# Quartering the value weights of an attention and experts kernel and loading them ahead of a block of x

## Chip, cores and metric

One core of a Trainium2 chip. The metric is the device time of one execution in microseconds (us); less is better.

## What is computed

One transformer layer on x of 2048 rows by 512 columns, in f32: attention and then a mixture of experts, each followed by a residual sum and a layer norm. Only the start matters here, the projections:

```python
q = (x @ Wq + bq).reshape(B, T, H, HD)
k = (x @ Wk + bk).reshape(B, T, HKV, HD)
v = (x @ Wv + bv).reshape(B, T, HKV, HD)
```

H is 16, HKV is 4 and HD is 128, so that Wv is 512 by 512.

## The kernel before, in words

`stage_project` is the first of the stages; after it come attention, the router, the experts and the last layer norm. Each of the five engines has one instruction stream, and semaphores join them. Within a stream the order is written by hand and is strict: an instruction behind a wait does not start before that wait is met.

**The split.** Each f32 matrix product is done as three products of halves: every operand is split into a high part, a rounded copy (ScalarE, `nc.scalar.copy`), and a low part, the value less its high part (VectorE, a subtraction). TensorE sums low by high, high by low and high by high in PSUM.

**The blocks.** x goes through in 16 blocks of 128 rows, called block 0 to block 15 below. For each, SyncE loads it (256 KB) into `xraw[k]`, k being the block's parity; TensorE transposes it in four pieces (`transposes`, L234, instructions at L239); ScalarE writes the high part (`x_hi`, L305, instruction at L311); VectorE the low part (`x_lo`, L392, L394) and keeps it for the later stage (`keep_lo`, L397, L399); GpSimd keeps the high part (`keep_hi`). Then twelve products with the value weights follow (`project_v`, L242, at L248), a bias (L405), a split (L317, L409) and a store of 512 KB (`store_v`, L177).

**The value weights.** `wv_raw` is 128 by 2048: four chunks of 512 columns, one for each 128 columns of x. It is loaded in two halves of 512 KB (L170), split in two halves (L324 and L417), and the products of block 0 are written by themselves (`project_first`, L252, at L258 with the high parts of the weights and at L263 with the low ones).

**TensorE's order at the start** (L267 to L275): 7 matmuls on zeros that keep the array busy (`keep_busy`, L103, each showing as two instructions of the trace at L106), transposes of blocks 0 and 1, 15 more `keep_busy`, the products of block 0, the transposes of block 2, the products of block 1. Then a loop: transposes of block 3, products of 2, transposes of 4, products of 3, and so on.

**SyncE's order** (L165 to L192): the identity (64 KB), blocks 0 and 1 of x, the two halves of the value weights, the bias `bv_b` (256 KB); blocks 2 and 3, each behind a wait for the transposes of the block that held its buffer (`xt_done`, L174); two head weights `w_raw` (257 KB each), `cosT` and `sinT` (1024 KB each), the mask (64 KB); and in a loop from there block 4, the store of block 0's values, block 5, the store of block 1's values, and so on. `load_x(4)` waits for three transposed blocks. The tables `cosT` and `sinT` are first read at L444, in the stage's second part, which starts at 60 us.

Of the kernel before, what the change touches and what calls it, by code (L numbers as in the profile page):

```python
# [23 lines left out]
F32 = mybir.dt.float32  # L24
# [5 lines left out]
ALU = mybir.AluOpType  # L30
# [3 lines left out]
P = 128  # L34
T = 2048
C = 512
# [6 lines left out]
NC = C // P  # L43
# [3 lines left out]
HI, LO = 0, 1  # L47
# [55 lines left out]
def keep_busy(nc, n, bank, ident):  # L103

    for _ in range(n):
        nc.tensor.matmul(bank, ident, ident, start=True, stop=True)  # L106


def stage_project(nc, base, own, sems, passed, x, wqk, wv, bv, cos, sin, ident_d, mask_d, qk_d, v_d):
    NH = H + HKV  # L110
    with ExitStack() as ctx:
# [5 lines left out]
        def sem(name):  # L117
            return sems.enter_context(nc.semaphore("p1_" + name))

        ident, maskf, identb, maskb = own.ident, own.maskf, own.identb, own.maskb  # L120
# [3 lines left out]
        xraw = [sb(f"xraw{k}", [P, C], kb=3 + 2 * k) for k in range(2)]  # L124
        xt = [[sb(f"xt{k}{s}", [P, NC, P], F32R) for s in "hl"] for k in range(2)]
        wv_raw = sb("wv_raw", [P, NC * C])
        wv_s = [sb(f"wv{s}", [P, NC * C], F32R) for s in "hl"]
        WV = [slice(s * NC * C // 2, (s + 1) * NC * C // 2) for s in range(2)]
        bv_b = sb("bv_b", [P, C])
        vfull = [sb(f"vfull{k}", [P, C]) for k in range(2)]  # L130
        vout = [sb(f"vout{k}", [P, HKV, 2, HD], F32R) for k in range(2)]
# [18 lines left out]

        x_in = [sem(f"x_in{k}") for k in range(2)]
        ident_in, const_in, bv_in = own.ident_in, sem("const_in"), sem("bv_in")
        wv_in = [sem(f"wv_in{s}") for s in range(2)]
        wv_hi, wv_lo = sem("wv_hi"), sem("wv_lo")
        xt_done, xt_hi, xt_lo = sem("xt_done"), sem("xt_hi"), sem("xt_lo")
        hi_kept, lo_kept = sem("hi_kept"), sem("lo_kept")
# [7 lines left out]

        def sync(sp, preload):  # L165
            sp.dma_start(ident[:], ident_d).then_inc(ident_in, 16)
            for k in range(2):
                sp.dma_start(xraw[k][:], x[k * P:(k + 1) * P, :]).then_inc(x_in[k], 16)
            for s in range(2):
                sp.dma_start(wv_raw[:, WV[s]], wv[:, WV[s]]).then_inc(wv_in[s], 16)  # L170
            sp.dma_start(bv_b[:], bv.partition_broadcast(P)).then_inc(bv_in, 16)

            def load_x(tb, k):
                sp.wait_ge(xt_done, tb - 1)  # L174
                sp.dma_start(xraw[k][:], x[bass.ds(tb * P, P), :]).then_inc(x_in[k], 16)

            def store_v(tb, k):  # L177
                sp.wait_ge(v_lo, tb + 1)
                sp.dma_start(v_d[bass.ds(tb, 1)].rearrange("o j p h d -> p (o j) h d"),
                             vout[k][:].bitcast(F32)).then_inc(v_out[k], 16)  # L180

            for k in range(2):
                load_x(2 + k, k)
            for k in range(2):
                sp.dma_start(w_raw[k][:], wqk[k]).then_inc(w_in[k], 16)
            sp.dma_start(cosT[:], cos).then_inc(const_in, 16)
            sp.dma_start(sinT[:], sin).then_inc(const_in, 16)
            sp.dma_start(maskf[:], mask_d).then_inc(own.mask_in, 16)
            with sp.Fori(2, NB // 2) as i:
                for k in range(2):  # L190
                    load_x(i * 2 + k, k)
                    store_v(i * 2 + (k - 4), k)  # L192
            for tb in range(NB - 4, NB):
                store_v(tb, tb % 2)

            def head_step(i, between=(), last=False):
                for k in range(2):
                    n = i * 2 + k
                    if not last:
                        sp.wait_ge(w_lo, n + 1)  # L200
                        sp.dma_start(w_raw[k][:], wqk[bass.ds(n + 2, 1)].rearrange("o p m -> (o p) m")
                                     ).then_inc(w_in[k], 16)
                    if k < len(between) and between[k]:
                        between[k](sp)
                    for t in range(NT):
                        sp.wait_ge(q_lo, n * NT + (t + 1))
                        sp.dma_start(qk_d[bass.ds(n, 1), :, t].rearrange("o p h t -> (o p) h t"),
                                     qout[k][:, t].bitcast(F32)).then_inc(q_out[k], 16)

            with sp.Fori(0, EARLY // 2) as i:  # L210
                head_step(i)

            def keys(sp):
                for k in range(2):
                    sp.wait_ge(v_out[k], 16 * (NB // 2))
                    sp.wait_ge(q_out[k], 16 * NT * (EARLY // 2))
                preload[0](sp)

            head_step(EARLY // 2, (keys, preload[1]))
            head_step(EARLY // 2 + 1, (preload[2], preload[3]))  # L220
            head_step(EARLY // 2 + 2, (preload[4],))
            with sp.Fori(EARLY // 2 + 3, NH // 2 - 1) as i:
                head_step(i)
            def queries(sp):
                sp.wait_ge(q_out[0], 16 * NT * (NH // 2))
                preload[5](sp)

            head_step(NH // 2 - 1, (None, queries), last=True)
# [4 lines left out]
        def tensor(pe):  # L233
            def transposes(tb, k, i, early):  # L234
                pe.wait_ge(x_in[k], i * 16 + 16)
                if not early:
                    pe.wait_ge(xt_lo, tb - 1)
                for c in range(NC):
                    last = nc.tensor.transpose(pt[k][:, c, :], xraw[k][:, c * P:(c + 1) * P], ident[:])  # L239
                last.then_inc(xt_done, 1)  # L240
# [8 lines left out]
                                                start=(n == 0 and c == 0), stop=(n == 2 and c == NC - 1))  # L249
                last.then_inc(v_mm, 1)  # L250

            def project_first():  # L252
                pe.wait_ge(xt_lo, 1)
                for part in range(2):
                    pe.wait_ge(wv_hi, part + 1)
                    for xs in (HI, LO):
                        for c in range(part * NC // 2, (part + 1) * NC // 2):
                            nc.tensor.matmul(pv[0][:], xt[0][xs][:, c, :], wv_s[HI][:, c * C:(c + 1) * C],  # L258
                                             start=(c == 0 and xs == HI), stop=False)
                for part in range(2):  # L260
                    pe.wait_ge(wv_lo, part + 2)
                    for c in range(part * NC // 2, (part + 1) * NC // 2):
                        last = nc.tensor.matmul(pv[0][:], xt[0][HI][:, c, :], wv_s[LO][:, c * C:(c + 1) * C],  # L263
                                                start=False, stop=(c == NC - 1))
                last.then_inc(v_mm, 1)

            pe.wait_ge(wv_lo, 1)  # L267
            keep_busy(nc, 7, pq[0][:, 0:P], rs[0][:, 0:P])
            pe.wait_ge(ident_in, 16)
            transposes(0, 0, 0, True)  # L270
            transposes(1, 1, 0, True)
            keep_busy(nc, 15, pq[0][:, 0:P], ident[:])
            project_first()
            transposes(2, 0, 1, False)
            project_v(1, 1, True)  # L275
            with pe.Fori(1, NB // 2 - 1) as i:
# [27 lines left out]
        def scalar(act):  # L304
            def x_hi(tb, k, early):  # L305
                act.wait_ge(xt_done, tb + 1)
                if not early:
                    act.wait_ge(v_mm, tb - 1)
                    act.wait_ge(hi_kept, tb - 1)
                    act.wait_ge(lo_kept, tb - 1)  # L310
                nc.scalar.copy(xt[k][HI][:], pt[k][:]).then_inc(xt_hi, 1)  # L311
# [5 lines left out]
                nc.scalar.copy(vout[k][:, :, HI, :], vfull[k][:].rearrange("p (j d) -> p j d", j=HKV)  # L317
                               ).then_inc(v_hi, 1)

            for k in range(2):  # L320
                x_hi(k, k, True)
            for s in range(2):
                act.wait_ge(wv_in[s], 16)
                nc.scalar.copy(wv_s[HI][:, WV[s]], wv_raw[:, WV[s]]).then_inc(wv_hi, 1)  # L324
            for k in range(2):
                x_hi(2 + k, k, False)
                v_hi_part(k, k, 0, True)
# [33 lines left out]
                v_hi_part(NB - 2 + k, k, NB // 2 - 1, False)  # L361
            act.wait_ge(ident_in, 16)
            nc.scalar.copy(identb[:], ident[:]).then_inc(own.mask_ready, 1)
            act.wait_ge(own.mask_in, 16)
            nc.scalar.copy(maskb[:], maskf[:]).then_inc(own.mask_ready, 1)

            def head_step(i, first, last=False):
# [21 lines left out]
        def vector(dve):  # L389
            nc.vector.memset(rs[0][:, 0:P], 0.0).then_inc(wv_lo, 1)  # L390

            def x_lo(tb, k):  # L392
                dve.wait_ge(xt_hi, tb + 1)
                nc.vector.tensor_tensor(xt[k][LO][:], pt[k][:], xt[k][HI][:].bitcast(F32), ALU.subtract  # L394
                                        ).then_inc(xt_lo, 1)

            def keep_lo(tb, k):  # L397
                dve.wait_ge(xt_lo, tb + 1)
                nc.vector.tensor_copy(xT[LO][:, :, bass.ds(tb * P, P)], xt[k][LO][:].bitcast(F32)).then_inc(lo_kept, 1)  # L399
# [9 lines left out]
                nc.vector.tensor_tensor(vout[k][:, :, LO, :], vfull[k][:].rearrange("p (j d) -> p j d", j=HKV),  # L409
                                        vout[k][:, :, HI, :].bitcast(F32), ALU.subtract).then_inc(v_lo, 1)  # L410

            for k in range(2):
                x_lo(k, k)
                keep_lo(k, k)
            for s in range(2):
                dve.wait_ge(wv_hi, s + 1)
                nc.vector.tensor_tensor(wv_s[LO][:, WV[s]], wv_raw[:, WV[s]], wv_s[HI][:, WV[s]].bitcast(F32), ALU.subtract  # L417
                                        ).then_inc(wv_lo, 1)
            dve.wait_ge(bv_in, 16)

            def step(i, first):
# [39 lines left out]
            for k in range(2):  # L461
                v_bias(NB - 2 + k, k, False)
                v_lo_part(NB - 2 + k, k)
            dve.wait_ge(const_in, 32)

            def head_step(i, first, last=False):
                for k in range(2):
# [1782 lines left out]
```

## Time and profile before

| What | us |
|---|---|
| Median of 3 runs | 2062.01 (2060.47 to 2062.39) |
| The profiled execution's own time | 2060.34 |
| Its span in the trace | 2058.5 |
| TensorE busy | 2038.4, 99% of the span |
| VectorE, ScalarE, GpSimd busy | 1691.4, 1400.6, 854.4 |

The span is the part of an execution that the profiler covers. PE is TensorE, PEld its weight loads, DVE is VectorE, ACT is ScalarE, POOL is GpSimd, SPq are the DMA issues of SyncE. A row of the timeline gives the start, the length of the merged stretch, the engine, the line, the tiles and the count; in brackets stands the idle time before it and what ended that. "DMA to landing" is the time from a transfer's issue to its semaphore. Ends of matmuls are modelled, so that the start of the next one is the better measure of what a group takes.

### The profile page before, as it was taken

Reading aid. Unit: us, or ns where it says so; the run is one execution under the profiler, and the core shown is the slowest. Engines: PE = TensorE matmul, PEld = TensorE weight load, DVE = VectorE, ACT = ScalarE, POOL = GpSimd, SP = SyncE. Lnnn points to the kernel's source line nnn. Section 1 sums busy time; section 2 is a strip of 40 time slices with the busy share of each in tenths; the row PEclk is TensorE's granted clock in tenths of the full one; section 3 lists DMA queues with packets and bytes.
Section 4 is the critical chain, followed back from the end, with each engine's and each line's share of the span. In section 5 each row is a group of like instructions: output and inputs, shape, how many; then the busy total and the mean of one; then the engine's idle time right before and its main releaser. Section 6 shows DMA issues by size and latency. Waiting matters only on the chain.

```text
span 2058.5 us, 36148 instructions
## 1 busy us (share of the span) xinstructions
PE 2038.4 (99%) x11961; PEld 1745.4 (85%) x11961; DVE 1691.4 (82%) x3508; ACT 1400.6 (68%) x2726; POOL 854.4 (42%) x812
## 2 busy tenths in 40 slices
PE   9999999999999999999999999999989999999998
PEld 8888888888888888888888888788879999999997
DVE  6899997888778887788877888566678889898886
ACT  3677776776667666677667776433447778777876
POOL 1000023333233332333323333155557777788775
PEclk9999999999999999999999999999999999999999
DMA  7458564011340213402243010567649999999998
GB/s 268 184 219 293 222 233 147 26 72 44 129 146 21 73 53 125 141 21 72 77 170 133 22 72 25 199 244 285 241 158 258 298 295 298 302 288 296 302 292 269
DMA packets 130405, 361.07 MB, mean 175 GB/s; under 512 B 15312, under 2 KB 32208, under 8 KB 125648
## 3 DMA queue, kind: packets, MB, share of 16 engines
q1 hardware_dynamic: 102160, 292.03, 40.1%
q0 software_dynamic: 28096, 67.12, 13.7%
q8 instruction: 85, 1.39, 0.3%
q14 instruction: 64, 0.52, 0.1%
HBM read 224.21 MB, written 134.89 MB: 174 GB/s over the span
## 4 chain that ended last, share of the span: by engine, by line
PE 81%; DVE 3%; ACT 2%; issue 1%; DMA 0%; POOL 0%; DVEq 0%; ACTq 0%; POOLq 0%
PE p_S L724 18%; PE p_O L756 17%; PE p_TP L738 11%; PE p_pgu L1678 9%; PE p_acc L1147 8%; PE p_prest L1678 4%; PE p_py L1695 4%; PE p_tp L1663 3%; PE p_py L1696 1%; PE p_py L1697 1%; ACT p_prob L822 1%; PE p_lg L1169 1%; ACT p_pT1h L830 1%; DVE p_nmax L879 1%; PE p_picked L1708 1%
## 5 line engine op out<-in xcount | busy, mean ns | idle before, releaser
L724 PE MATMUL p_S<-p_kT,p_q 128*128 128x512 f32 (+3 forms) x1920 | 459.6, 369 | 1.0
L724 PEld LDWEIGHTS p_S<-p_kT,p_q 128*128 128x128 f32 x1920 | 333.7, 188 | 66.3 <-ACT p_prob L822 14.7
L948 POOL TENSOR_SCALAR p_prob<-p_prob,p_inv 128x256 f32<-128x256 f32 (+7 forms) x256 | 193.1, 754 | 432.8 <-DVE p_inv L890 432.7
L948 POOL TENSOR_SCALAR p_prob<-p_prob,p_inv,p_part 128x1024 f32<-128x1024 f32 (+1 forms) x128 | 150.8, 1178 | 455.2 <-DVE p_inv L895 455.2
L879 DVE TENSOR_REDUCE p_nmax<-p_S 128x1 f32<-128x1024 f32 (+6 forms) x256 | 253.6, 991 | 80.7 <-PE p_S L724 74.3
L738 PE MATMUL p_TP<-p_ident,p_prob 128*128 128x128 f32 x2176 | 307.6, 273 | 2.0 <-DVE p_pT0l L900 1.1
L738 PEld LDWEIGHTS p_TP<-p_ident,p_prob 128*128 128x128 f32 x2176 | 250.7, 140 | 45.9 <-issue 11.8
L830 ACT CAST p_pT1h<-p_TP 128x512 fp32r<-128x512 f32 (+2 forms) x320 | 164.9, 552 | 98.2 <-PE p_TP L738 98.1
L830 ACT CAST p_pT0h<-p_TP 128x384 fp32r<-128x384 f32 (+3 forms) x320 | 147.8, 498 | 117.3 <-PE p_TP L738 117.1
L1945 POOL DMA_INDIRECT sum_scratch<-p_y,p_tokT x124 | 206.0, 1661 | 42.6 <-issue 37.2
L756 PE MATMUL p_O<-p_pT1h,p_v 128*128 128x512 f32 x584 | 222.1, 411 | 0.4 <-DVE p_pT1l L900 0.2
L822 ACT ACTIVATE p_prob<-p_S,p_nm 128x256 f32<-128x256 f32 (+7 forms) x256 | 189.7, 741 | 38.8 <-DVE p_nm L879 36.1
L900 DVE TENSOR_TENSOR p_pT1l<-p_TP,p_pT1h 128x512 fp32r<-128x512 f32 (+2 forms) x320 | 197.2, 633 | 20.0 <-ACT p_pT1h L830 18.2
L1933 POOL DMA_INDIRECT p_xg<-x_scratch,p_tokT x128 | 168.5, 1317 | 75.0 <-issue 38.1
L756 PE MATMUL p_O<-p_pT0h,p_v 128*128 128x512 f32 x504 | 194.4, 413 | 0.0
L900 DVE TENSOR_TENSOR p_pT0l<-p_TP,p_pT0h 128x384 fp32r<-128x384 f32 (+3 forms) x320 | 175.8, 566 | 13.8 <-ACT p_pT0h L830 13.4
L1147 PE MATMUL p_acc<-p_woh,p_ot 128*128 128x512 f32 x512 | 172.4, 402 | 0.0
L822 ACT ACTIVATE p_prob<-p_S,p_nmax 128x1024 f32<-128x1024 f32 (+1 forms) x128 | 142.4, 1112 | 4.9 <-DVE p_nmax L879 1.8
L879 DVE TENSOR_REDUCE p_nm<-p_S 128x1 f32<-128x128 f32 (+7 forms) x128 | 96.3, 753 | 51.3 <-PE p_S L727 50.5
L756 PEld LDWEIGHTS p_O<-p_pT1h,p_v 128*128 128x128 f32 x584 | 110.0, 188 | 19.4 <-DVE p_pT1l L900 1.4
L1511 POOL TENSOR_SCALAR p_lo_hot<-p_iota_lo,p_lo 128x128 f16<-128x128 f32 x117 | 77.8, 683 | 88.2 <-DVE p_hi L1403 88.2
L756 PE MATMUL p_O<-p_pT1l,p_v 128*128 128x512 f32 x292 | 114.3, 392 | 0.0
(356 smaller groups left out, 4567.0 us busy)
## 6 DMA issues: line engine op xcount, KB each, us to landing
p_w_raw<-in_gu SPq DMA_DIRECT2D x64, 768.0 KB, 7.0
qk_scratch<-p_qout SPq DMA_DIRECT2D x80, 512.0 KB, 2.7
p_q<-qk_scratch SPq DMA_DIRECT2D x16, 2048.0 KB, 8.8
o_scratch<-p_oT SPq DMA_DIRECT2D x64, 512.0 KB, 3.3
p_ot<-o_scratch SPq DMA_DIRECT2D x32, 1024.0 KB, 7.2
p_w_raw<-in_gu SPq DMA_DIRECT2D x64, 256.0 KB, 8.3
v_scratch<-p_vout SPq DMA_DIRECT2D x16, 512.0 KB, 2.9
p_t_raw<-in_dn SPq DMA_DIRECT2D x32, 256.0 KB, 8.0
```

The costliest lines, as they stand in the source:

```text
L724: mm = nc.tensor.matmul(out if k0 // 512 == (k1 - 1) // 512 else out.rearrange("p (n k) -> p n k", n=2), x, y, start=(n == 0), stop=(n == 2))
L738: mm = nc.tensor.transpose(TP[g % 2][:, n, :], prob[u % KEEP][:, s * P:(s + 1) * P], ident[:])
L756: mm = nc.tensor.matmul(O[f % 2][:], x, y, start=(s == 0 and i == 0), stop=(s == nblk(f) - 1 and i == 2))
L822: nc.scalar.activation(prob[k][:, keys(u, a)], S[:, score_cols(u, a)], ACT.Exp, bias=top[:, k:k + 1], accum_out=rsum[:, k, a:a + 1]).then_ ...
L830: nc.scalar.copy(pT[m % 2][HI][:, 0:n, g, :], TP[g % 2][:, 0:n, :]).then_inc(turn_hi, 1)
L879: r = nc.vector.reduce_max(out[:, k:k + 1], S[:, cols], AX_X, negate=True)
L900: nc.vector.tensor_tensor(pT[m % 2][LO][:, 0:n, g, :], TP[g % 2][:, 0:n, :], pT[m % 2][HI][:, 0:n, g, :].bitcast(F32), ALU.subtract).then_ ...
L948: nc.gpsimd.tensor_scalar(prob[k][:, cols], prob[k][:, cols], inv[:, k:k + 1], scale, ALU.mult, ALU.mult).then_inc(normed, 1)
L1147: mm = nc.tensor.matmul(acc[k][:], a, w, start=(n == 0 and m == 0), stop=(n == H - 1 and m == 2))
L1678: mm = nc.tensor.matmul(out, a[:, col:col + P], b[:, d, :], start=(m == 0 and d == 0), stop=(m == 2 and d == NC - 1))
L1933: nc.gpsimd.indirect_dma_start(out=xg[k][c][:], out_offset=None, in_=x1_d, in_offset=bass.IndirectOffsetOnAxis(ap=tokT[:, e, c:c + 1], axi ...
L1945: nc.gpsimd.indirect_dma_start(out=sum_d[k], out_offset=bass.IndirectOffsetOnAxis(ap=tokT[:, e, c:c + 1], axis=0), in_=y[k][c][:], in_offs ...
```

## The change

The value weights are loaded, split and multiplied in four quarters of 256 KB, `WV[c]` now being chunk c. Block 1 of x is loaded behind them. ScalarE and VectorE split block 1 behind the four quarters. TensorE's order becomes: 7 `keep_busy`, transposes of block 0, 8 `keep_busy`, the products of block 0 chunk by chunk (for each chunk two with its high part, and one with the low part of the chunk before), the transposes of block 1 ahead of the last low product, and then transposes of block 2 and products of block 1 as before. SyncE waits for the four high parts (`wv_hi`) ahead of `cosT`. Since quarters 2 and 3 signal `const_in` and `mask_in`, the later waits on these count 16 more. The diff, without its lines of context:

```diff
--- before.py
+++ after.py
...
-        WV = [slice(s * NC * C // 2, (s + 1) * NC * C // 2) for s in range(2)]
+        WV = [slice(c * C, (c + 1) * C) for c in range(NC)]
...
-        wv_in = [sem(f"wv_in{s}") for s in range(2)]
+        wv_in = [sem(f"wv_in{s}") for s in range(2)] + [const_in, own.mask_in]
...
-            for k in range(2):
-                sp.dma_start(xraw[k][:], x[k * P:(k + 1) * P, :]).then_inc(x_in[k], 16)
-            for s in range(2):
-                sp.dma_start(wv_raw[:, WV[s]], wv[:, WV[s]]).then_inc(wv_in[s], 16)
+            sp.dma_start(xraw[0][:], x[0:P, :]).then_inc(x_in[0], 16)
+            for c in range(NC):
+                sp.dma_start(wv_raw[:, WV[c]], wv[:, WV[c]]).then_inc(wv_in[c], 16)
+            sp.dma_start(xraw[1][:], x[P:2 * P, :]).then_inc(x_in[1], 16)
...
+            sp.wait_ge(wv_hi, NC)
...
-            def project_first():
+            def first_high(c):
...
-                for part in range(2):
-                    pe.wait_ge(wv_hi, part + 1)
-                    for xs in (HI, LO):
-                        for c in range(part * NC // 2, (part + 1) * NC // 2):
-                            nc.tensor.matmul(pv[0][:], xt[0][xs][:, c, :], wv_s[HI][:, c * C:(c + 1) * C],
-                                             start=(c == 0 and xs == HI), stop=False)
-                for part in range(2):
-                    pe.wait_ge(wv_lo, part + 2)
-                    for c in range(part * NC // 2, (part + 1) * NC // 2):
-                        last = nc.tensor.matmul(pv[0][:], xt[0][HI][:, c, :], wv_s[LO][:, c * C:(c + 1) * C],
-                                                start=False, stop=(c == NC - 1))
-                last.then_inc(v_mm, 1)
+                pe.wait_ge(wv_hi, c + 1)
+                for xs in (HI, LO):
+                    nc.tensor.matmul(pv[0][:], xt[0][xs][:, c, :], wv_s[HI][:, WV[c]], start=(c == 0 and xs == HI), stop=False)
+
+            def first_low(c):
+                pe.wait_ge(wv_lo, c + 2)
+                mm = nc.tensor.matmul(pv[0][:], xt[0][HI][:, c, :], wv_s[LO][:, WV[c]], start=False, stop=(c == NC - 1))
+                if c == NC - 1:
+                    mm.then_inc(v_mm, 1)
...
+            keep_busy(nc, 8, pq[0][:, 0:P], ident[:])
+            first_high(0)
+            for c in range(1, NC):
+                first_high(c)
+                first_low(c - 1)
...
-            keep_busy(nc, 15, pq[0][:, 0:P], ident[:])
-            project_first()
+            first_low(NC - 1)
...
-            for k in range(2):
-                x_hi(k, k, True)
-            for s in range(2):
-                act.wait_ge(wv_in[s], 16)
-                nc.scalar.copy(wv_s[HI][:, WV[s]], wv_raw[:, WV[s]]).then_inc(wv_hi, 1)
+            x_hi(0, 0, True)
+            for c in range(NC):
+                act.wait_ge(wv_in[c], 16)
+                nc.scalar.copy(wv_s[HI][:, WV[c]], wv_raw[:, WV[c]]).then_inc(wv_hi, 1)
+            x_hi(1, 1, True)
...
-            act.wait_ge(own.mask_in, 16)
+            act.wait_ge(own.mask_in, 32)
...
-            for k in range(2):
-                x_lo(k, k)
-                keep_lo(k, k)
-            for s in range(2):
-                dve.wait_ge(wv_hi, s + 1)
-                nc.vector.tensor_tensor(wv_s[LO][:, WV[s]], wv_raw[:, WV[s]], wv_s[HI][:, WV[s]].bitcast(F32), ALU.subtract
+            x_lo(0, 0)
+            for c in range(NC):
+                dve.wait_ge(wv_hi, c + 1)
+                nc.vector.tensor_tensor(wv_s[LO][:, WV[c]], wv_raw[:, WV[c]], wv_s[HI][:, WV[c]].bitcast(F32), ALU.subtract
...
+                if c == 0:
+                    keep_lo(0, 0)
+            x_lo(1, 1)
+            keep_lo(1, 1)
...
-            dve.wait_ge(const_in, 32)
+            dve.wait_ge(const_in, 48)
```

## Rows read from the trace of the kernel before

**Rows 1.** The page: busy us of each engine (share of the span).

```profile
PE 2038.4 (99%) x11961; PEld 1745.4 (85%) x11961; DVE 1691.4 (82%) x3508; ACT 1400.6 (68%) x2726; POOL 854.4 (42%) x812
```

**Rows 2.** TensorE's waits from 20 to 1300 us: total, times, longest.

```profile
PE p_TP L738 <- DVE p_pT0l L900: 1.1, 6, 0.3
PE p_TP L738 <- DVE p_pT1l L900: 0.7, 1, 0.7
```

**Rows 3.** Timeline from 0 to 14 us: start, us, engine, line, tiles.

```profile
1.06 3.35 PE L106 MATMUL p_pq<-p_rs 128*128 128x128 f32 x14 [1.06 <-DVE p_rs L390]
...
4.20 1.15 PE L239 MATMUL p_pt<-p_ident,p_xraw 128*128 128x128 f32 x8
...
4.91 0.58 ACT L311 CAST p_xt0h<-p_pt 128x512 fp32r<-128x512 f32 x1 [2.89 <-PE p_pt L239]
...
5.18 3.51 PE L106 MATMUL p_pq<-p_ident 128*128 128x128 f32 x30
...
5.53 0.69 DVE L394 TENSOR_TENSOR p_xt0l<-p_pt,p_xt0h 128x512 fp32r<-128x512 f32 x1 [4.53 <-ACT p_xt0h L311]
...
6.25 0.87 DVE L399 CAST p_xTl<-p_xt0l 128x512 fp32r<-128x512 f32 x1
...
8.40 1.04 ACT L324 CAST p_wvh<-p_wv_raw 128x1024 fp32r<-128x1024 f32 x1 [2.42 <-DMA p_wv_raw<-in_wv]
9.48 2.47 DVE L417 TENSOR_TENSOR p_wvl<-p_wv_raw,p_wvh 128x1024 fp32r<-128x1024 f32 x2 [1.29 <-ACT p_wvh L324]
...
9.59 0.70 PE L258 MATMUL p_pv<-p_wvh,p_xt0h 128*128 128x512 f32 x2 [0.90 <-ACT p_wvh L324]
...
11.80 1.08 PE L263 MATMUL p_pv<-p_wvl,p_xt0h 128*128 128x512 f32 x4
...
12.72 0.60 PE L239 MATMUL p_pt<-p_ident,p_xraw 128*128 128x128 f32 x4
...
13.07 1.18 PE L248 MATMUL p_pv<-p_wvh,p_xt1l 128*128 128x512 f32 x4
```

**Rows 4.** Timeline of SyncE's DMA issues from 0 to 14 us.

```profile
1.19 0.90 SPq L168 DMA_DIRECT2D p_xraw<-in_x  x2
...
4.91 1.08 SPq L175 DMA_DIRECT2D p_xraw<-in_x  x2
...
8.22 0.50 SPq L188 DMA_DIRECT2D p_maskf<-in_mask  x1
13.51 0.35 SPq L175 DMA_DIRECT2D p_xraw<-in_x  x1
```

**Rows 5.** Loads of x by tile: block 0; blocks 0, 1; blocks 2, 3; block 4.

```profile
DMA to landing us min/median/max: 2.6/2.6/2.6
...
DMA to landing us min/median/max: 2.6/2.8/3.0
...
DMA to landing us min/median/max: 6.0/6.1/6.2
...
DMA to landing us min/median/max: 5.1/5.1/5.1
```

**Rows 6.** Loads of the value weights by tile: the first half; both halves.

```profile
DMA to landing us min/median/max: 6.3/6.3/6.3
...
DMA to landing us min/median/max: 6.3/6.6/7.0
```

**Rows 7.** Timeline, TensorE's transposes of blocks 3 and 4.

```profile
15.93 0.60 PE L239 MATMUL p_pt<-p_ident,p_xraw 128*128 128x128 f32 x4
...
19.13 0.60 PE L239 MATMUL p_pt<-p_ident,p_xraw 128*128 128x128 f32 x4
```

**Rows 8.** Busy us by window: PE, PEld, DVE, ACT, POOL, PEclk, DMA share, GB/s.

```profile
1541.00:1542.00 1.00, 0.00 (x0) 0.00 (x0) 0.45 (x2) 0.46 (x1) 0.81 (x1) 1.00 0.67 255
...
2052.00:2054.00 2.00, 0.00 (x0) 0.00 (x0) 1.79 (x7) 1.85 (x4) 0.00 (x0) 1.00 0.66 253
2054.00:2056.00 2.00, 0.00 (x0) 0.00 (x0) 0.48 (x1) 0.52 (x1) 0.00 (x0) 0.94 0.95 369
```

## The prediction

> **What bounds the kernel now.** I read the page first: TensorE is busy for 2038.4 us, 99% of the span [rows 1]. Then its waits: between 20 and 1300 us they come to 1.8 us in all, none over 0.7 [rows 2]. So there is next to no slack in which a shift of TensorE's start could vanish. Whatever the change does to the moment at which TensorE enters its steady work on the blocks of x moves the end by as much, and it can do nothing else, for it touches only the first 20 us or so. The whole question lies in the start, so I read its timeline next.
>
> Up to 4.20 us TensorE runs filler; then come the transposes of blocks 0 and 1, and filler again. The first products wait 0.90 us for the high part of the value weights, whose first half ScalarE can't copy before 8.40; block 0's products last until 12.72, and block 1's begin at 13.07 [rows 3]. The landings say why: block 0 of x arrives at 1.19 + 2.6 = 3.8 and block 1, issued 0.45 later, at 1.64 + 3.0 = 4.6 [rows 4, 5]. The weights' two issues follow at 2.1 and 2.6 in SyncE's order, and land 6.3 and 7.0 us later, at 8.4 and 9.6 [rows 6]. From 13.07 on TensorE goes without a gap: transposes of blocks 3 and 4 start 3.20 us apart, at 15.93 and 19.13 [rows 7].
>
> The last thing to read is how near the loads are to being late. Blocks 2 and 3, issued at 4.91 and 5.4, land at 10.9 and 11.6. Block 4 is issued at 13.51, behind both head weights, both tables and the mask, and lands at 18.6 [rows 4, 5]. TensorE transposes it at 19.13 [rows 7]. That leaves 0.5 us of slack, in a queue that has been full since the start.
>
> **The change, part by part.** *Loads.* The same bytes go through the queue up to block 2; block 1 (256 KB) only trades places with the weights (1024 KB). I therefore read landings by the bytes ahead of them. Quarter 0 takes block 1's old place, 4.6. Quarters 1 and 2 fill the first half's old place: quarter 2 at 8.4 and quarter 1 about midway, 6.5. Quarter 3 is midway to the second half, 9.0, and block 1 is last, at 9.6. That two more transfers cost nothing by themselves I take from blocks 2 and 3: 256 KB each, 0.7 us apart. The upper bound for quarter 3 is that it lands no sooner than the second half did, 9.6; the lower is that it gains a whole 1.2 (9.6 less 8.4), 8.4.
>
> *Filler and block 0.* Seven fillers go (14 instructions at 3.51/30 = 0.12 us, 1.6 us); they were waiting time filled up, and what ends the wait is the weights, so they are worth nothing. Eight fillers last from 4.6 to 6.4. Quarter 0 is split by then (copy 4.9 to 5.5 for block 0, then 0.58 for the quarter), and block 0's low part is ready at 6.22 [rows 3]. A 512-column copy takes 0.58 and a subtraction 0.69 [rows 3]; a matmul with 512 columns takes (12.72 - 11.80)/4 = 0.23, and four transposes 13.07 - 12.72 = 0.35 [rows 3]. Quarter 3's high part is ready at 9.0 + 0.6, say 9.7 with quarter 2's copy just ahead and the signals. Two high products and a low one bring TensorE to 10.4, transposes of block 1 to 10.75, the last low product to 11.0. Block 0 so ends 1.7 us sooner than 12.72. VectorE's `keep_lo` of 0.87 behind quarter 0 lies in the gap before quarter 1's high part and delays a low product at most.
>
> *Block 1.* This is what takes most of that back. Its transposes used to be done by 5.4; now their results are out at 10.75 + 0.25 = 11.0 (a group of 0.60 whose successor starts after 0.35). ScalarE then needs 0.58 and VectorE 0.69, with some 0.05 for each signal: block 1's products can start at 12.45. TensorE has the transposes of block 2 (11.0 to 11.35; its data landed at 10.9) to fill that, and stands for 1.1 us. Against 13.07 the gain at this point is 0.6 us. Unhindered, blocks 3 and 4 would be transposed at 15.3 and 18.5.
>
> *SyncE's queue.* `load_x(3)` waits for two transposed blocks. It used to pass at 5.3 and now passes at 11.1. Behind it in the stream stand both head weights, cos, sin, the mask, and then block 4. The new wait on `wv_hi` ahead of cos is met at 9.7 and costs nothing. But the queue, full until now, runs dry at about 10.9, when block 2 has landed, and the next data start only with an issue at 11.1. Block 3 then lands like the one load that had an almost empty queue, 2.6 later [rows 5]: 13.7, ahead of its 15.3. From block 3's landing to block 4's it took 18.6 - 11.6 = 7.0 us for 2881 KB, at an unbroken pace; nothing in the change shortens it. Block 4 then lands at 20.7. TensorE wants it at 18.5, waits 2.3 us and transposes it at 20.8, where it was 19.13: **1.65 us later**. Next in the queue are the store of block 0's values and block 5, 768 KB, 1.9 us at that pace, so 22.6, and TensorE wants block 5 at 20.8 + 3.2 = 24.0: no second stall. The tables land near 20, against a first use at 60.
>
> In short, from the moment t at which block 1's transposes are out, block 4 is ready at t + 0.1 + 2.6 + 7.0, and before it was used at 19.13: the loss is t - 9.4, with t = 11.0. The bounds: t from 10.4 to 11.6 (quarter 3 at 8.4 or 9.6), and 2.6 may be 3.0 (block 1's), so +1.0 to +2.6. If block 4 isn't late at all, -0.6 stays.
>
> *Clock.* TensorE ran its first filler, 14 instructions, in 3.1 us and the later in half the time each [rows 3]: the lower level, 1.2 GHz, and then 2.4. The rise comes with the same 7 fillers as before. Ahead of me are idle stretches of 1.1 and 2.3 us and a half-idle one from 6.4 to 9.7. In the trace, an empty microsecond (1541 to 1542) kept 1.00; at the end, with 2052 to 2054 empty, it was 1.00 still and fell only within the next two [rows 8]. So my sum has no loss here. The Trainium skill, TensorE: Matmul & The Clock Gate, Part 1: The HAM clock gate, says that sustained work releases the throttle and idleness brings it back. By that rule this change trades away cover: the idle stretch could cost the lower clock behind it. The rows agree as to the end of the kernel and show no fall after a short gap.
>
> The sum: 2062.01 + 1.65 = 2063.7. Against the profiled execution, 2060.34, it is 2062.0; that execution was 1.7 below the median, and I forecast the median.
>
> **The rivals.** (a) *Only the gain stays.* Block 4 comes in time: the 18.5 of TensorE holds, and the time is 2062.0 - 0.6 = 2061.4. For it: the weights may come much faster once block 1 is out of the way, since the 3.8 us between 4.6 and 8.4 for the first half is three times the 1.2 for the second. Against it: t enters both TensorE's want and block 4's landing, so that some stall remains whenever the queue runs dry; to gain on balance t has to be under 9.4. (b) *The change doesn't do what it says*: quarter 3 lands with the old second half, at 9.6, because the slowest of the DMA engines sets every landing. Then t is 11.6 and the loss 2.2: 2064.2. Against it: landings by bytes were even from 8.4 on. (c) *Slower, by the clock.* The 2.3 us without a matmul ahead of block 4's transposes, or the half-idle start, lets the clock fall to 1.2 GHz. From the first filler, 3.1 us at the lower level do 1.6 us of work, so one such stretch costs 1.6: 2065.3. Two make it 2066.9, which is slower by more than 0.2%. It decides from an idle stretch longer than those that kept 1.00, over 2 us and up to 4.
>
> **How the numbers follow.** A measurement of this kernel can tell about 0.2%, 4.1 us, from no change. Chances: the forecast 0.60; (a) 0.20; (b) 0.10; (c) 0.10, of which 0.03 for two stretches. All but the last lie within 4.1 us. So same 0.95; slower 0.04, with 0.01 for something in the loads that I can't see; faster 0.01, as nothing here is worth 4.1 us. The range: the forecast with its bounds is 2063.0 to 2064.6; (a) draws it to 2061.4; the median of three runs moved within 2060.5 to 2062.4, about 1 us each way. 2060.9 to 2065.3 leaves out (c) with two stretches and the tails.
>
> **What would show it.** Right: block 0's last low product near 11 us, `xraw`'s fourth load issued at about 11, a wait of TensorE (or its weight loads) for block 4 of x of some 2 us near 18.5 to 20.8, and `keep_busy` gone from 6.4 on. Transposes of block 4 at 20.8 settle the sum, as all behind them is rigid. Wrong: those transposes before 19.13; then look at when `load_x(3)` was issued and whether the queue ran dry. Clock under 1.00 in windows before 30 us is rival (c). If the end moves by more than those transposes do, the cause is outside this argument.

## The result, and the profile after

| | us |
|---|---|
| Changed kernel, median of 8 runs | 2067.71 (2066.60 to 2069.27) |
| Kernel before, 8 runs beside it | 2060.94 (2058.79 to 2062.54) |
| Ratio | 1.0034, 95% interval 1.0025 to 1.0042 |
| Profiled execution, and its span | 2068.74, 2066.9 |

The change makes the kernel slower by 6.8 us, more than the 4.1 us that I had called the limit of no change, and beyond the upper end of my range. The page, against [rows 1]:

```profile
span 2066.9 us, 36129 instructions
...
PE 2041.0 (99%) x11947; PEld 1747.3 (85%) x11947; DVE 1691.0 (82%) x3510; ACT 1401.6 (68%) x2728; POOL 856.9 (41%) x812
```

TensorE is busy 2.6 us longer with 14 instructions fewer: the first hint of a lower clock. Its timeline from 5 to 34 us (idle time before in brackets), against [rows 3, 7]:

```profile
5.06 2.08 PE L106 MATMUL p_pq<-p_ident 128*128 128x128 f32 x16
...
9.52 0.47 PE L257 MATMUL p_pv<-p_wvh,p_xt0h 128*128 128x512 f32 x1 [1.22 <-ACT p_wvh L325]
...
10.99 0.60 PE L240 MATMUL p_pt<-p_ident,p_xraw 128*128 128x128 f32 x4
...
12.99 1.20 PE L249 MATMUL p_pv<-p_wvh,p_xt1l 128*128 128x512 f32 x4 [0.73 <-DVE p_xt1l L396]
...
15.87 0.60 PE L240 MATMUL p_pt<-p_ident,p_xraw 128*128 128x128 f32 x4
...
24.69 1.12 PE L240 MATMUL p_pt<-p_ident,p_xraw 128*128 128x128 f32 x4 [5.45 <-DMA p_xraw<-in_x]
25.46 2.06 PE L249 MATMUL p_pv<-p_wvh,p_xt1l 128*128 128x512 f32 x4
27.31 1.91 PE L249 MATMUL p_pv<-p_wvl,p_xt1h 128*128 128x512 f32 x4
29.02 1.17 PE L249 MATMUL p_pv<-p_wvh,p_xt1h 128*128 128x512 f32 x4
30.02 0.60 PE L240 MATMUL p_pt<-p_ident,p_xraw 128*128 128x128 f32 x4
...
33.23 0.60 PE L240 MATMUL p_pt<-p_ident,p_xraw 128*128 128x128 f32 x4
```

Up to 16 us the forecast and the trace agree within 0.6 us. Then TensorE stands for 5.45 us until block 4 of x has landed, and works at half pace behind that. Block 4's transposes are at 24.69 for 19.13 (5.6 us later); block 5's at 30.02, which is 5.33 behind them where the spacing before was 3.20 (2.1 us more). From there the spacing is 3.21 again. In the kernel before, block 5's transposes stood here:

```profile
22.34 0.60 PE L239 MATMUL p_pt<-p_ident,p_xraw 128*128 128x128 f32 x4
```

So 7.7 us are lost by 30 us. The rest of the kernel carries that on: followed instruction by instruction, VectorE and ScalarE lag the trace of before by 7.7 us at 100 us and by 8.0 at 1500. What is left to explain is where these two terms come from.

SyncE's issues (start, length, count) say when block 3's and block 4's loads went out, against [rows 4]:

```profile
5.30 6.66 SPq L175 DMA_DIRECT2D p_xraw<-in_x  x2
11.99 0.91 SPq L185 DMA_DIRECT2D p_w_raw<-in_wqk  x2
12.95 0.43 SPq L187 DMA_DIRECT2D p_cosT<-in_cos  x1
...
14.70 0.35 SPq L175 DMA_DIRECT2D p_xraw<-in_x  x1
```

The landings by tile of block 3 (issued at 11.6) and block 4, against [rows 5]:

```profile
DMA to landing us min/median/max: 2.5/2.5/2.5
...
DMA to landing us min/median/max: 9.9/9.9/9.9
```

Block 3 lands at 14.1 and block 4 at 24.6: from one to the other, with the head weights, tables and mask between them, it takes 10.5 us where it took 7.0. By their landings the two head weights take 4.0 of these (1.3 before) and the tables 5.7 (4.9 before). The windows (columns as in [rows 8]) give the queue and the clock:

```profile
10.00:12.00 2.00, 2.00 (x14) 1.65 (x13) 0.71 (x2) 0.37 (x1) 0.00 (x0) 1.00 0.06 24
12.00:14.00 2.00, 1.27 (x7) 0.89 (x6) 1.72 (x4) 0.80 (x2) 1.34 (x2) 1.00 0.67 196
14.00:16.00 2.00, 2.00 (x11) 1.58 (x10) 1.62 (x3) 0.62 (x1) 0.00 (x0) 1.00 0.99 270
...
22.00:23.00 1.00, 0.00 (x0) 0.00 (x0) 0.00 (x0) 0.00 (x0) 0.00 (x0) 0.69 1.00 363
23.00:24.00 1.00, 0.00 (x0) 0.00 (x0) 0.00 (x0) 0.00 (x0) 0.00 (x0) 0.50 1.08 394
...
28.00:29.00 1.00, 1.00 (x3) 0.73 (x3) 0.57 (x2) 0.62 (x1) 0.00 (x0) 0.50 0.09 33
29.00:30.00 1.00, 1.00 (x5) 0.80 (x4) 0.35 (x1) 0.00 (x0) 0.00 (x0) 0.89 0.00 0
```

The queue ran dry from 10 to 12 (DMA share 0.06), as forecast, though a whole microsecond ahead of block 2's landing (11.3), by which the forecast reckoned; and it came back at 196 and 270 GB/s. The granted clock fell to its lower level, 1.2 GHz, during the idle stretch and came back in the window from 29 to 30.

### The profile page after: what moved, and what is told of

Same layout as the page of the kernel before. It is cut to its first block, busy times and chain, and to the rows that moved or that the text cites. A ratio compares the mean times of both kernels' runs of the same rounds, so it can differ in the third digit from the quotient of the medians.

```text
span 2066.9 us, 36129 instructions
## 1 busy us (share of the span) xinstructions
PE 2041.0 (99%) x11947; PEld 1747.3 (85%) x11947; DVE 1691.0 (82%) x3510; ACT 1401.6 (68%) x2728; POOL 856.9 (41%) x812
## 4 chain that ended last, share of the span: by engine, by line
PE 81%; DVE 3%; ACT 2%; issue 1%; DMA 0%; POOL 0%; DVEq 0%; ACTq 0%; POOLq 0%
PE p_S L728 18%; PE p_O L760 17%; PE p_TP L742 11%; PE p_pgu L1682 9%; PE p_acc L1151 8%; PE p_prest L1682 4%; PE p_py L1699 4%; PE p_tp L1667 3%; PE p_py L1700 1%; PE p_py L1701 1%; ACT p_prob L826 1%; PE p_lg L1173 1%; ACT p_pT1h L834 1%; DVE p_nmax L883 1%; PE p_picked L1712 1%
```

## Experiments

Each kernel is given as its edit against the kernel named. Ratios are to the kernel before, beside it on the same chip.

**hold_only** asks whether the held load of block 3 alone does it, without quarters.

```diff
-            for k in range(2):
-                load_x(2 + k, k)
+            load_x(2, 0)
+            sp.wait_ge(wv_lo, 3)
+            load_x(3, 1)
```

> The kernel before, with one wait added: SyncE issues block 3's load of x only when VectorE has split the second half of the value weights (near 12 us; in the kernel before it went out at 5.4). Theory H (the held-back load lets the queue run dry, and block 4 comes behind 2.6 MB of head weights and tables): block 4 lands at 24 to 25 us, as with the change, where it was 18.6; TensorE stands for over 5 us ahead of its transposes, the granted clock falls to 0.50 for some microseconds behind that, and the time is 5 to 8 us over the kernel before. Rival Q (the quarters of the value weights, with their short rows and more transfers, are what slows the loads): block 4 lands near 18.6 plus the hold's own gap, under 21, the clock stays at 1.00 and the time is within 2 us of the kernel before.

2068.6 us, ratio 1.0036 (1.0023 to 1.0048). TensorE's row for block 4, block 4's landing, and a window behind it:

```profile
23.26 1.11 PE L240 MATMUL p_pt<-p_ident,p_xraw 128*128 128x128 f32 x4 [4.85 <-DMA p_xraw<-in_x]
```

```profile
DMA to landing us min/median/max: 9.0/9.0/9.0
```

```profile
24.00:26.00 2.00, 2.00 (x7) 1.61 (x6) 0.81 (x2) 0.59 (x1) 0.60 (x1) 0.50 0.88 305
```

Block 4 issued at 14.2 lands at 23.2. A kernel with the value weights in halves and one wait more loses what the change loses. Rival Q falls; SyncE's hold is the cause. The clock costs 2.4 us here: block 5's transposes come 5.60 us behind block 4's (28.86 less 23.26).

**quarters_only** is the other part alone: the changed kernel with block 1 put back ahead of the weights on SyncE, TensorE, ScalarE and VectorE.

```diff
-            sp.dma_start(xraw[0][:], x[0:P, :]).then_inc(x_in[0], 16)
+            for k in range(2):
+                sp.dma_start(xraw[k][:], x[k * P:(k + 1) * P, :]).then_inc(x_in[k], 16)
...
-            sp.dma_start(xraw[1][:], x[P:2 * P, :]).then_inc(x_in[1], 16)
```

> The changed kernel with block 1 of x put back where it was: loaded, transposed and split ahead of the value weights, which stay in four quarters. Theory H: block 3's load goes out at about 5.5 again, block 4 lands at 18.6, no clock loss; the products of block 1 start 1 to 1.5 us before the kernel before's 13.07, near 11.8, but block 4's landing at 18.6 against a want of about 17.9 gives most of it back: 0.3 to 0.8 us faster than the kernel before. Rival Q: the quarters keep the cost, 5 us or more slower than the kernel before.

2061.7 us, ratio 1.0007 (0.9998 to 1.0017). TensorE's timeline:

```profile
10.93 1.18 PE L249 MATMUL p_pv<-p_wvh,p_xt1l 128*128 128x512 f32 x4
...
20.37 0.66 PE L240 MATMUL p_pt<-p_ident,p_xraw 128*128 128x128 f32 x4 [3.23 <-DMA p_xraw<-in_x]
```

Block 1's products start at 10.93 for 13.07, a better start than I expected; but block 4 lands at 20.3, not 18.6, and the clock falls behind the wait (4.83 us to block 5's transposes at 25.20), so theory H was wrong on both. All is given back, and in this trace more: block 5's transposes are 2.9 us late, while the median is 0.6 us above the kernel before and the ten runs spread from 2059.1 to 2065.3. The wait on `wv_hi`, which I had priced at nothing, is met here at 9.3, and the tables' issue moves there from 7.2.

**fill_stall** takes the idleness away and leaves the late load.

```diff
-            with pe.Fori(1, NB // 2 - 1) as i:
+            transposes(3, 1, 1, False)
+            project_v(2, 0, False)
+            keep_busy(nc, 20, pq[0][:, 0:P], ident[:])
+            transposes(4, 0, 2, False)
+            project_v(3, 1, False)
+            with pe.Fori(2, NB // 2 - 1) as i:
```

> The changed kernel with 20 keep_busy (40 instructions of the trace, some 4.7 us at full clock) ahead of the transposes of block 4, in the place where TensorE stands idle for 5.45 us; the loop's first turn is written out for that. It takes the idleness away and leaves the late load. Theory C (the idle stretch lets the clock fall, and that costs 2.1 us behind it): the granted clock stays at 1.00 between 22 and 30 us, block 5's transposes start 3.2 us behind block 4's instead of 5.3, and the time is about 2.1 us under the changed kernel. Rival (the lower clock is only seen there, the late chain behind block 4 sets the pace anyway): same time as the changed kernel within 0.7 us.

2066.03 us, ratio 1.0024 (1.0014 to 1.0034), against the changed kernel's 1.0034: some 2 us less, though these two ratios come from separate comparisons and their intervals overlap, so that the gain in time is likely and not shown by itself.

```profile
24.05 0.66 PE L240 MATMUL p_pt<-p_ident,p_xraw 128*128 128x128 f32 x4 [0.43 <-DMA p_xraw<-in_x]
27.29 0.60 PE L240 MATMUL p_pt<-p_ident,p_xraw 128*128 128x128 f32 x4
```

```profile
24.00:26.00 2.00, 1.96 (x11) 1.70 (x12) 0.49 (x1) 0.59 (x1) 0.27 (x1) 1.00 0.98 355
```

The clock stays at 1.00 and the spacing is 3.24 where it was 5.33: this the trace does show. The idle stretch itself costs the 2.1 us; filler that does no work buys them back.

**cos_early** is meant to keep the queue from running dry. The head weight's semaphore counts cosT's load as well.

```diff
-            for k in range(2):
-                load_x(2 + k, k)
+            load_x(2, 0)
+            sp.dma_start(cosT[:], cos).then_inc(w_in[0], 16)
+            load_x(3, 1)
...
-            sp.dma_start(cosT[:], cos).then_inc(const_in, 16)
```

> The changed kernel with the 1 MB load of cosT issued ahead of block 3's held load (behind block 2's), so that the queue has work until about 13.4 us and never runs dry; the bytes are the same. Theory D (the gap in the queue is what costs: the idle time itself and a slow restart behind it): block 4 lands at 18.6 to 19.2, TensorE waits under 1 us for it, the clock stays at 1.00 and the time is within 1 us of the kernel before. Rival O (it is the issue of many transfers at once, or the order of these transfers, not the gap, that makes the pace slow): block 4 still lands at 22 us or later and 4 us or more of the loss stay.

2063.94 us, ratio 1.0011 (1.0002 to 1.0021). It falls between the two: block 4 lands at 21.0.

```profile
21.07 1.12 PE L240 MATMUL p_pt<-p_ident,p_xraw 128*128 128x128 f32 x4 [2.21 <-DMA p_xraw<-in_x]
25.89 0.60 PE L240 MATMUL p_pt<-p_ident,p_xraw 128*128 128x128 f32 x4
```

```profile
11.00:12.00 1.00, 0.87 (x7) 0.56 (x5) 0.15 (x1) 0.68 (x2) 0.01 (x1) 1.00 0.66 279
...
22.00:24.00 2.00, 2.00 (x6) 1.61 (x6) 1.01 (x2) 0.58 (x1) 0.61 (x1) 0.50 0.84 282
```

Theory D as I put it is not borne out: block 4 is 2 us later than it allowed. Nor was its condition met: the DMA share was 0.66 from 11 to 12 already, ahead of cosT's landing at 13.4. Rival O (22 us or later, 4 us or more left) isn't borne out either. Yet 4 of the 6.8 us are gone. Here an idle stretch of 2.21 us went with the fall to 0.50, and cost 1.6 us more (4.82 between the blocks for 3.20).

**many_issues** tests whether issuing transfers slows those that move (EXTRA is 8).

```diff
+            sp.wait_ge(wv_hi, 1)
+            for j in range(EXTRA):
+                sp.dma_start(qout[0][:, 0, HI, j * 16:(j + 1) * 16].bitcast(F32), cos[:, j * 16:(j + 1) * 16]
+                             ).then_inc(ident_in, 16)
```

> The kernel before with eight more transfers of 8 KB each (a bit of the cos table into a buffer that is free until 60 us), issued by SyncE from about 9.5 to 13.2 us, behind the mask's and ahead of block 4's; their data is 64 KB in all and comes behind the mask's in the queue. Only the landings of cosT and sinT are read, which are ahead of it all. In the kernel before they land at 15.3 and 17.8, 2.5 us apart. Theory I (what makes the pace slow is that SyncE issues transfers while the data ahead are moving): cosT and sinT land later, together by 1 us or more. Theory S (some stretch of the data itself is slow, or the queue's restart): both land where they did, within 0.3 us, and at most block 4 comes up to 1 us later for the eight small transfers' own data.

cosT, issued at 7.5, lands at 15.0, and sinT, at 8.2, lands at 17.5, 2.5 us apart. Theory I falls.

**tables_late** leaves block 3 and the head weights early and holds the tables alone; **tables_mid** holds them less (`wv_hi`, 1); **tables_late_cut** is tables_late with each table as four column parts. These three and many_issues ran once each (2063.1, 2061.7, 2066.5 and 2063.0 us) and are read by their traces.

```diff
+            sp.wait_ge(wv_lo, 3)
             sp.dma_start(cosT[:], cos).then_inc(const_in, 16)
```

> The kernel before with one wait added ahead of cosT's issue, until VectorE has split the second half of the value weights (near 12 us); block 3 and both head weights stay early, so that the queue has data until about 12.9 and block 4 has the same bytes ahead of it. If the pace of the tables is slow only behind a queue that has run dry or because they are issued shortly ahead of their data (short lead), cosT and sinT take over 6 us together from the second head weight's landing and block 4 lands at 20 or later; if it were only the held block 3 that mattered, they take 5 and block 4 lands at 18.6 to 19.2.

> The kernel before with the wait ahead of cosT's issue on the first half of the value weights' high part (met near 9.4 us), between the 7.2 us of the kernel before and the 11.6 us of tables_late. Theory L (the pace of a transfer falls with the lead of its issue over its data): cosT and sinT take between 5.0 us (before) and 7.6 us (tables_late) from the second head weight's landing, near 6 to 7, as in quarters_only (7.0, issued at 9.3). Theory G (only a queue without work behind the head weights does it): they take 5.0 to 5.3, since the queue has data until 12.9 us.

> tables_late with each table issued as four column parts of 256 KB (rows of 2 KB for rows of 8 KB), eight transfers in all, from 11.6 us on. Theory L (lead alone): still some 7 us or more from the second head weight to the last part of sinT. Theory W (the long rows, read in step by all DMA engines, are what stalls): 5.0 to 5.6 us.

| | tables issued | second head weight lands | sinT lands | both tables take | block 4 lands |
|---|---|---|---|---|---|
| before | 7.2 | 12.9 | 17.8 | 4.9 | 18.6 |
| tables_mid | 8.9 | 12.9 | 17.8 | 4.9 | 18.6 |
| tables_late | 11.6 | 12.5 | 20.2 | 7.7 | 21.2 |
| tables_late_cut | 13.0 | 13.9 | 23.7 | 9.8 | 24.6 |

A shorter lead alone costs nothing (tables_mid), so theory L falls as a matter of degree; short rows make nothing better (tables_late_cut), so W falls. (The landings are the issue's start plus the time to landing, by tile, to 0.1 us.)

Three windows of tables_late, then one of the kernel before with the tables in full flow:

```profile
11.00:12.00 1.00, 1.00 (x6) 0.83 (x5) 0.56 (x1) 0.00 (x0) 0.00 (x0) 1.00 0.70 267
12.00:13.00 1.00, 1.00 (x9) 0.82 (x8) 0.00 (x0) 0.06 (x1) 0.00 (x0) 1.00 0.91 133
13.00:14.00 1.00, 1.00 (x6) 0.82 (x5) 0.36 (x1) 0.53 (x1) 0.21 (x1) 1.00 0.61 229
```

```profile
13.00:14.00 1.00, 1.00 (x7) 0.86 (x6) 0.00 (x0) 0.59 (x1) 0.00 (x0) 1.00 0.99 418
```

Three things go with the slow pace. First, part of the DMA engines stop having work: the share is 0.70 from 11 to 12, though the second head weight lands only at 12.5, so that the queue need not look empty by its landings. Second, and this no landing shows, they are slow when they start again: from 12 to 13 the engines are busy 0.91 of the time and move 133 GB/s. In the trace's DMA records that window holds 16 packets of the tables (8 KB each), at 0.9 us each; in full flow one takes 0.31. Over the whole loads, none of the 256 such packets took over 0.5 us in either trace of the kernel before or in many_issues, 5 did in tables_mid, 18 in tables_late and in hold_only, 33 and 35 in the two traces of the changed kernel. Third, the engines drift apart, and a landing waits for the last. Behind block 4 stands the store of block 0's values (the first packets of 1 KB); of such packets 243 KB had started before block 4's landing in the kernel before, 546 KB in the changed one.

quarters_only is mostly the third thing: only 6 packets over 0.5 us, nine tenths of the tables' packets started by 16.1 (15.8 in the kernel before), but the last at 18.9 (17.1), and 767 KB of stores started before block 4's landing. What makes a packet slow behind a pause, and what sets the engines apart, stays open. That the pause is what brings it on is my reading: it fits tables_mid against tables_late, and no run varies the pause alone.

**before_again** and **after_again** repeat the two kernels for a second trace.

> The kernel before once more, for a second trace of it. If its head weights and tables go at an even pace by their place in the queue, block 3 lands within 0.5 us of 11.6, cosT near 15.3 and block 4 near 18.6 again, 7.0 us behind block 3; if that pace is a matter of luck, these move by 1 us or more.

> The changed kernel once more, for a second trace of it. If the 10.5 us between block 3's and block 4's landing belong to the late issue, they are 9 to 11 again (hold_only had 9.4, fill_stall 9.8); if they were luck, they are nearer to 7. The granted clock falls behind the idle stretch again, to 0.50. The second stretch of 0.50 at 1551 us, which other traces of other kernels have or lack, may be there or not; where it is not, the span is 2 us shorter.

before_again: block 3 lands at 11.6, cosT at 15.4, block 4 at 18.6, as before. after_again: block 4, issued at 14.5, lands at 24.0, 9.8 us behind block 3, late again; TensorE stands 4.96 us, and block 5's transposes are at 28.88, so that the clock costs 1.7 us. The lateness belongs to the kernel and not to the run. Where it shows does not: here the head weights take 1.6 us and the tables 7.4, for 4.0 and 5.7 in the first trace.

A wait late in the kernel concerns another thing. TensorE's row behind it and a window in before_again, then the row in hold_only:

```profile
1542.19 0.66 PE L1663 MATMUL p_tp<-p_ident,p_xg 128*128 128x128 f32 x4 [2.11 <-DMA p_xg<-x_scratch,p_tokT]
```

```profile
1544.00:1546.00 2.00, 2.00 (x11) 2.00 (x11) 0.75 (x1) 0.00 (x0) 1.00 (x1) 0.50 0.71 151
```

```profile
1549.12 0.66 PE L1664 MATMUL p_tp<-p_ident,p_xg 128*128 128x128 f32 x4 [2.17 <-DMA p_xg<-x_scratch,p_tokT]
```

The clock falls near 1543 us in this run of the kernel before too; the run is level with the first trace up to 1540 us and 1.5 us behind it at 1550. In hold_only the same wait, as long, left the clock at 1.00. Of the twelve traces in which this wait lasted over 2 us, six have the fall (2.04 to 2.29 us, the changed kernel's two among them) and six have not (2.08 to 2.19). So it comes and goes with the run, and some 1.5 us of the difference between the first two spans (8.4) are not the change's.

**The repair.** Since everything hangs on block 4's place, three kernels take the head weights and tables out of its way, the tables in four column parts each: `before_spread`, `after_spread` (changed kernel) and `quarters_spread` (quarters_only).

```diff
             for k in range(2):
                 load_x(2 + k, k)
...
+            for tb in range(4, NB):
+                load_x(tb, tb % 2)
+                if tb < 6:
+                    sp.dma_start(w_raw[tb - 4][:], wqk[tb - 4]).then_inc(w_in[tb - 4], 16)
+                elif tb < 14:
+                    tab, src = (cosT, cos) if tb < 10 else (sinT, sin)
+                    cols = slice((tb - 6) % 4 * 512, (tb - 6) % 4 * 512 + 512)
+                    sp.dma_start(tab[:, cols], src[:, cols]).then_inc(const_in, 16)
+                elif tb == 14:
+                    sp.dma_start(maskf[:], mask_d).then_inc(own.mask_in, 16)
+                store_v(tb - 4, tb % 2)
```

> The kernel before, with SyncE's order changed alone: blocks 4 and 5 of x ahead of the head weights, the two tables cut into four column parts of 256 KB each and issued one behind each load of blocks 6 to 13, the mask behind block 14; SyncE's loop is written out. Block 4 lands by 16 us. Since TensorE had no wait behind 13 us before, no time is to be gained: within 0.5 us of the kernel before, unless the load now and then came late in runs without a profile (then up to 1 us faster, with less scatter).

> The changed kernel with that same order of SyncE. Theory H (all of the loss hangs on block 4's place behind 2.6 MB in the queue): block 4 lands near 15 us, ahead of its want at 18.5 to 18.9, no idle stretch and no clock loss, transposes of block 4 at 18.9 against 19.13 before: 0 to 0.6 us faster than the kernel before, some 6.5 us faster than the changed one. Rival (something else in the change costs too): 1 us or more slower than the kernel before.

> The run quarters_only (four quarters, block 1 of x ahead of them) with that same order of SyncE. Its products of block 1 began at 10.93 us against 13.07 in the kernel before, and its transposes of block 4 waited 3.23 us for data. With block 4 landing near 15 they start at 17.0 against 19.13: 2.1 us faster than the kernel before, if no later load is late; if a load is late each time by some tenths, 1 to 2 us faster.

> quarters_spread once more, to narrow its interval. Its trace entered the steady work 2.1 us earlier than the kernel before's; the first comparison gave 0.9994 (0.9985 to 1.0003). If the early start reaches the end, the ratio is near 0.9992 again (1 to 2 us); if it is lost on the way, 1.0000.

| | median | before beside it | ratio (95%) | block 4's transposes |
|---|---|---|---|---|
| before_spread | 2060.98 | 2061.57 | 0.9997 (0.9988 to 1.0006) | 19.02 |
| after_spread | 2061.66 | 2061.57 | 1.0003 (0.9994 to 1.0012) | 18.45 |
| quarters_spread | 2060.18 | 2061.57 | 0.9994 (0.9985 to 1.0003) | 17.34 |
| quarters_spread_again | 2057.96 | 2059.83 | 0.9993 (0.9984 to 1.0002) | 17.32 |

after_spread is the test of the whole account: the changed kernel with SyncE's order alone altered has no wait for block 4 and loses nothing measurable. Its products, splits, borrowed semaphores and the held block 3 are all still there. In quarters_spread the steady work starts earlier by 1.8 us (not by the 2.1 that the expectation of its repeat names):

```profile
17.34 0.60 PE L242 MATMUL p_pt<-p_ident,p_xraw 128*128 128x128 f32 x4
```

Twice its median is 1.4 and 1.9 us under the kernel before. Each interval alone still touches 1.0, so I call it likely and not shown that the gain reaches the end.

## Why the prediction was wrong

**Bounding by the start: right.** The loss at block 5's transposes (7.7 us in one trace, 28.88 - 22.34 = 6.5 in the other) is the loss in the medians (6.8), and in both traces the lag changes by less than 0.4 us from 100 to 1500 us.

**Landings by the bytes ahead: right enough.** Quarter 3 landed at 3.1 + 6.3 = 9.4 (forecast 9.0), block 1 at 10.0 (9.6), block 2 at 11.3 (10.9). Block 1's transposes began at 10.99 for 10.4, t was 11.6 for 11.0, the upper bound that I gave; block 1's products began at 12.99 for 12.45. The sum hung t on quarter 3; in the trace TensorE ran without a gap from quarter 2's high products, at 9.52, to block 1's transposes, so that quarter 2 (landed at 8.7 for 8.4) set it. The gain of 0.6 us at that point shrank to 0.1, with rival (b)'s t but not by its cause, for quarter 3 didn't land with the old second half (9.6).

**SyncE's queue: the mechanism right, a term mis-sized.** The step that failed reads: "From block 3's landing to block 4's it took 18.6 - 11.6 = 7.0 us for 2881 KB, at an unbroken pace; nothing in the change shortens it." Nothing lengthened it in my sum either. I gave bounds to t and to block 3's 2.6 us, and none to this, the largest term, though I had just written that the queue would run dry ahead of it. It was 10.5, 9.8 in the second trace, and 9.4 in hold_only. The rows before held a warning: the start, the one other place where the DMA engines begin from nothing, took 3.8 us from block 1's landing to the first half's for 512 KB, three times the 1.2 of the second half; and that trace's windows show 227 to 330 GB/s from 2 to 9 us against 395 to 447 from 9 to 16. I used the first only in favour of rival (a), and did not read the second. Of 5.56 us at block 4: 1.65 forecast, 0.5 from block 3's issue (11.6 for 11.1), 3.5 from the pace, less about 0.1 for block 3's 2.5.

**Clock: wrong.** I put it at nothing in the sum and gave it 0.10, though my own sum had an idle stretch of 2.3 us in it. The row that I leaned on was one microsecond long, and the end of the kernel, where an empty window of 2 us still had 1.00, bounds no other place: the same 1541 to 1542 us lie in a wait of 1.62 us that lasted 2.11 in the second trace, and there the clock fell. cos_early fell behind 2.21 us, quarters_only behind 3.23. The rule that I cited from the Trainium skill, TensorE: Matmul & The Clock Gate, Part 1: The HAM clock gate, that idleness brings the throttle back, held here: granted clock 0.50 from 23 to 29 us, behind 5.45 us without a matmul. The price of one stretch in rival (c), 1.6, was near: 1.6 in cos_early and quarters_only, 1.7 and 2.1 in the two traces here, 2.4 in hold_only.

**The rivals and the range.** (b)'s later t and (c)'s clock both came on top of the forecast; I had treated them as alternatives, and they add. With the pace right, TensorE would still have stood some 2 us (5.45 less 3.5), and had the clock fallen behind that, 1.65 + 0.5 + 1.6 is an estimate of 3.8 us. A range over separate cases leaves out the case in which one brings on the next: a later load lengthens the idle stretch that costs the clock. The new wait on `wv_hi` cost nothing in the changed kernel (cosT follows the head weights at once, 12.95), as I said; with block 1 in front it does move the tables.

## What to carry to other kernels

Before a load is reordered, follow SyncE's stream past it: a wait that used to be met at 5 us and is now met at 11 holds up every transfer behind it, and the one that matters may be six places down, behind bulk data that nobody needs yet. Put what is needed at 60 us behind what is needed at 19, or in pieces between. And price a wait of an otherwise full TensorE at more than its length, for the clock may go with it; where the wait can't be removed, filler can keep the clock, as in the trace of fill_stall.

## What the runs showed of the hardware

- A DMA queue's pace after a pause was not its pace in full flow: two tables took 4.9 us with the queue full behind the head weights, 7.7 and 9.8 when they were issued as it emptied, whether in rows of 8 or of 2 KB. Neither a shorter lead (tables_mid) nor eight further issues (many_issues) did that. The DMA engines were not idle all that time: a packet of 8 KB took 0.31 us in full flow, and the 16 that started first behind the pause in tables_late (12 to 13 us) 0.9 us each.
- Landings hide how far the DMA engines are apart: in the changed kernel 546 KB of stores issued behind block 4's load had started before that load had landed.
- TensorE's granted clock fell to 0.50 behind idle stretches of 2.21, 2.34 (tables_late), 3.23, 4.31 (tables_late_cut), 4.85, 4.96 and 5.45 us, and stayed at 1.00 behind one of 0.43 (fill_stall) and 1.01 (many_issues). Behind the wait near 1542 us, 2.04 to 2.29 us long, it fell in six of twelve traces. In before_spread and quarters_spread_again it fell near 1520 us with no idle stretch over 1.2 us close by.
- From block 2 on, the landings in the kernel before repeated to 0.1 us in a second trace. That is not the rule: the second half of the value weights, issued alike, landed at 9.6 in both and at 9.2 in tables_late, 9.4 in many_issues and 10.6 in tables_late_cut. Block 4's slack of 0.5 us is less than such a load can move.
